# Scores of an attention block: operands of three bf16 parts, two heads per 128 rows, transposed scores as tiles of 64 rows

## The reference, cut to what matters

```python
Q = rope((x @ qw).reshape(b, s, 16, 8)); K = rope((x @ kw).reshape(b, s, 16, 8)); V = (x @ vw).reshape(b, s, 16, 8)
score = einsum('bhqd,bhkd->bhqk', Q, K) / sqrt(8) - 1e10 * (1 - causal)
weights = softmax(score - max(score))
x = layernorm(x + einsum('bhqk,bhkd->bhqd', weights, V).reshape(b, s, 128) @ ow)
gates = top-2 softmax of (x @ router_w + router_b)
x = layernorm(x + sum over experts e of gates[e] * ((silu(x @ w1[e]) * (x @ w3[e])) @ w2[e]))
```

## Time and profile before

| | |
|---|---|
| median of 3 runs | 478.48 us (477.96 to 478.5) |
| profiled execution | 479.53 us, its span 477.8 us |
| mean granted clock of TensorE | 0.955 |
| PE (TensorE matmul) busy | 444.2 us, 93% of the span |
| DVE (VectorE) busy | 318.8 us, 67% |
| ACT (ScalarE) busy | 276.5 us, 58% |
| POOL (GpSimd) busy | 167.2 us, 35% |
| chain that ended last | PE 75%, DVE 8%, ACT 5%, DMA 5%, issue 4% |

### The profile page before, as it was taken

The page is one execution under the profiler, slowest core; times in us unless marked ns, Lnnn a source line. Parts: engine busy times, 40 slices in busy tenths (PEclk is TensorE's granted clock), DMA queues, the critical chain, the costliest instruction groups (busy, mean ns, idle before and its releaser), DMA issues.

```text
span 477.8 us, 7339 instructions
## 1 busy us (share of the span) xinstructions
PE 444.2 (93%) x2340; PEld 278.9 (58%) x2340; DVE 318.8 (67%) x1059; ACT 276.5 (58%) x512; POOL 167.2 (35%) x167
## 2 busy tenths in 40 slices
PE   5877999999999999999999998989999999999991
PEld 2345555555545544545555544448887788788780
DVE  3889957777787787776867873314656756756753
ACT  1212056765766766757757656956566565665560
POOL 4514020240411502404205022026656555665661
PEclk9976579999999999999999999999999999999996
DMA  7977610312112303112122000000000000000000
GB/s 242 279 208 201 164 20 4 106 21 66 45 21 67 62 1 96 30 38 72 20 69 43 1 1 1 2 0 2 0 1 1 23 1 1 23 2 1 22 1 22
DMA packets 41749, 23.64 MB, mean 49 GB/s; under 512 B 31280, under 2 KB 33968, under 8 KB 41712
## 3 DMA queue, kind: packets, MB, share of 16 engines
q1 hardware_dynamic: 41712, 23.18, 17.8%
HBM read 14.26 MB, written 8.65 MB: 48 GB/s over the span
## 4 chain that ended last, share of the span: by engine, by line
PE 75%; DVE 8%; ACT 5%; DMA 5%; issue 4%; SPq 2%; POOL 0%; POOLq 0%; DVEq 0%; ACTq 0%
PE bank L968 16%; PE bank L984 16%; PE bank L1053 15%; PE bank L950 14%; PE bank L1064 7%; DVE maxima L718 3%; ACT num L545 3%; DVE num L777 2%; PE bank L1002 2%; PE bank L907 2%; DMA k_scratch<-rope_lo 2%; DVE num L850 2%; DMA q_scratch<-rope_lo 1%; ACT num L607 1%; SPq L325 1%
## 5 line engine op out<-in xcount | busy, mean ns | idle before, releaser
L545 ACT ACTIVATE num<-bank 128x512 f32<-128x512 f32 (+1 forms) x304 | 159.3, 579 | 98.4 <-PE bank L968 95.8
L950 PE MATMUL bank<-k_op,q_op 128*128 128x512 f32 (+15 forms) x384 | 126.9, 381 | 6.8 <-DMA q_op<-q_scratch 3.5
L968 PE MATMUL bank<-q_op,k_op 128*128 128x512 f32 (+1 forms) x304 | 129.8, 442 | 3.4 <-ACT num L545 2.3
L447 POOL TENSOR_SCALAR_AFFINE_SELECT num<-num 128x512 f32<-128x512 f32 x64 | 40.3, 636 | 214.1 <-ACT num L545 214.1
L718 DVE TENSOR_REDUCE maxima<-bank 128x1 f32<-128x512 f32 x128 | 87.7, 685 | 25.3 <-PE bank L950 24.6
L478 POOL TENSOR_TENSOR q_op<-num,q_op 128x512 fp32r<-128x512 f32 x64 | 82.9, 1299 | 60.4 <-ACT q_op L600 59.2
L950 PEld LDWEIGHTS bank<-k_op,q_op 128*128 128x128 f32 x384 | 76.0, 203 | 40.9 <-DVE maxima L718 23.0
L968 PEld LDWEIGHTS bank<-q_op,k_op 128*128 128x128 f32 x304 | 56.9, 191 | 65.1 <-ACT num L545 36.9
L984 PE MATMUL bank<-num,v_op 128*32 128x512 f32 (+3 forms) x768 | 82.5, 502 | 3.2 <-ACT num L545 2.5
L850 DVE TENSOR_TENSOR num<-bank,num 128x512 f32<-128x512 f32 x64 | 44.2, 691 | 56.9 <-ACT num L607 53.8
L1053 PE MATMUL bank<-q_op,w_hi 128*128 128x512 f32 x256 | 81.5, 400 | 0.4 <-DVE num L850 0.2
(11 more groups left out here) (87 smaller groups left out, 362.2 us busy)
## 6 DMA issues: line engine op xcount, KB each, us to landing
k_op<-k_scratch SPq DMA_DIRECT2D x16, 256.0 KB, 2.8
q_op<-q_scratch SPq DMA_DIRECT2D x64, 52.0 KB
w_raw<-in_w_all SPq DMA_DIRECT2D x6, 512.0 KB, 4.2
q_scratch<-rope_hi SPq DMA_DIRECT2D x8, 256.0 KB, 3.1
k_scratch<-rope_hi SPq DMA_DIRECT2D x8, 256.0 KB, 3.3
xT<-in_x_feat SPq DMA_DIRECT2D x4, 256.0 KB, 5.6
k_scratch<-k_op SPq DMA_DIRECT2D x2, 512.0 KB, 5.9
q_scratch<-rope_lo SPq DMA_DIRECT2D x4, 256.0 KB, 3.5
```

The source lines that it names most:

```text
L545: act.activation(num[:, t % PB, h:h + heads, off:CH], t_bank[k % TB][:, 0:heads * (CH - off)].rearrange("p (h t) -> p h t", h=heads), ACT. ...
L950: pe.matmul(s_bank[k % SB][:, 0:width], q_op[u][:, j, :, :].rearrange("p h q -> p (h q)"), k_op[u][:, lo:lo + width], start=True, stop=Tru ...
L968: pe.matmul(t_bank[k % TB][:, 0:heads * (CH - off)].rearrange("p (h j q) -> p h j q", h=heads, q=QD), k_op[w][:, kt * P:(kt + 1) * P], q_o ...
```

## The change

Q and K are kept in three bf16 parts. A head's operand has six products of parts, 48 rows, and three rows for the maximum; two heads stand on 128 rows (64 rows each), and a group of four heads takes two such pairs.

- The opening: for a chunk ScalarE rounds part 0, VectorE takes the rest in place, ScalarE rounds part 1 of the chunk before (`second_part`), GpSimd takes part 2 of the chunk two before (`third_part`). SP issues six stores of half the size for a chunk instead of three, and waits for part 0, 1 and 2 in turn. `load_k` has two DMAs instead of one. A memset of GpSimd moves behind its second chunk.
- S: 48 units again, 64 queries of two heads each; 17,408 columns in a stage instead of 16,896. Their banks, that of MROWS and that of NORM are now one ring of three (jobs, `JOB`, `ring`).
- T: a unit is 2 or 4 matmuls of 64 rows, the two heads of a pair on rows 0 to 63 and 64 to 127 and in two neighbouring banks; 20 units and 48 matmuls in a stage instead of 38 and 38. Two such double banks instead of three single ones. ScalarE takes one exponential of up to 1024 columns for a unit.
- PV: as before, one tile at a time; the buffers for its input are four instead of three.
- The split of the maxima, now in three parts, moves from VectorE to GpSimd, as five dependent operations; MROWS is a bf16 matmul.
- The plan's constants are set anew for the smaller number of T units.

```diff
-NB = CH // QD
+NPR = 2
+HR = P // NPR
+QB = P // NPR
+NB = CH // QB
 KT = S // P
-QROWS = 3 * DH + 2
-KROWS = 3 * DH
+Q_PART = (0, 0, 1, 1, 2, 0)
+K_PART = (0, 1, 0, 1, 0, 2)
+PARTS = 3
+KROWS = len(Q_PART) * DH
+QROWS = KROWS + PARTS
...
-S_UNITS = [(0, j, 0) for j in range(CH // QD)]
-S_UNITS += [(1, j, half) for j in range(CH // QD, S // QD) for half in range(2)]
+S_UNITS = [(j // NB, pr, j, half) for j in range(S // QB) for pr in range(NPR) for half in range(j // NB + 1)]
...
-    return CH // (CH - t_off(c, kt))
+    return 2 if CH - t_off(c, kt) > CH // 2 else GH
...
-TB = 3
+TB = 2
 HB = 4
-PB = 3
+PB = 4
...
-S_LATE, S_EARLY = 0, 3
-MROWS_AT, NORM_AT, MROWS0_AT, NORM0_AT = 5, 9, 18, 21
-PV_LAG, PV_LAG_LAST = 3, 6
+S_LATE, S_EARLY = 0, 2
+MROWS_AT, NORM_AT, MROWS0_AT, NORM0_AT = 2, 4, 9, 11
+PV_LAG, PV_LAG_LAST = 2, 3
...
+        job_bank = [low[0], low[1], small_bank]
+
+        def ring(s, step):
+
+            return small_bank if s == GROUPS else job_bank[JOB[s, step] % SB]
...
+                for part in range(PARTS):
+                    sp.wait_ge(part_ready[part], n + 1)
+                    for r, of in enumerate(K_PART if is_k else Q_PART):
+                        if of == part:
+                            sp.dma_start(dram[heads, r * DH:(r + 1) * DH, cols], rope_part[part][:, n % 2, :])\
+                                .then_inc(parts_stored[n % 2], 16)
...
+            def third_part(n):
+                pool.wait_ge(part_ready[1], n + 1)
+                if n >= 2:
+                    pool.wait_ge(parts_stored[n % 2], STORES * 16 * (n // 2))
+                pool.tensor_tensor(rope_part[2][:, n % 2, :], roped[:, n % 2, :], rope_part[1][:, n % 2, :],
+                                   ALU.subtract).then_inc(part_ready[2], 1)
 
             for n in range(2 * CHUNKS):
+                if n >= 2:
+                    third_part(n - 2)
                 pool.wait_ge(turned, n + 1)
                 if n >= 2:
-                    pool.wait_ge(lo_ready, n - 1)
+                    pool.wait_ge(part_ready[2], n - 1)
                 pool.tensor_tensor(roped[:, n % 2, :], by_cos[:, n % 2, :], by_sin[:, n % 2, :], ALU.add)\
                     .then_inc(roped_ready, 1)
-            pool.memset(flat[1].bitcast(F32), 0.0).then_inc(ops_filled, 1)
...
+            def split_max(s, c):
+
+                first = 5 * (NC * s + c)
+                top = maxima[:, 0, :, c * NB:(c + 1) * NB]
+
+                def then(ins, k):
+                    ins.then_inc(split_step, 1)
+                    pool.wait_ge(split_step, first + k)
+
+                if c > 0:
+                    pool.wait_ge(max_joined, s + 1)
+                else:
+                    pool.wait_ge(job_read, SB + last_score(s, c) + 1)
+                part = max_part[c]
+                then(pool.tensor_scalar(neg_max[:, :, :], top, -1.0, None, ALU.mult), 1)
+                then(pool.tensor_copy(part[:, :, 0, :], neg_max[:, :, :]), 2)
+                then(pool.tensor_tensor(rest[:, :, :], neg_max[:, :, :], part[:, :, 0, :], ALU.subtract), 3)
+                then(pool.tensor_copy(part[:, :, 1, :], rest[:, :, :]), 4)
+                then(pool.tensor_tensor(part[:, :, 2, :], rest[:, :, :], part[:, :, 1, :], ALU.subtract), 5)
+                pool.sem_inc(max_split, 1)
+
...
+            def second_part(n):
+                act.wait_ge(rest_ready, n + 1)
+                if n >= 2:
+                    act.wait_ge(parts_stored[n % 2], STORES * 16 * (n // 2))
+                act.activation(rope_part[1][:, n % 2, :], roped[:, n % 2, :], ACT.Copy).then_inc(part_ready[1], 1)
 
             for n in range(2 * CHUNKS):
+                if n == 4:
+                    act.wait_ge(ld_small, 16 * 2)
+                    act.activation(ident_b[:, :], ident[:, :], ACT.Copy).then_inc(ident_cast, 1)
                 if n in (PROJ_FIRST - 1, PROJ_FIRST + 1):
                     copy_v((n - PROJ_FIRST + 1) // 2)
                 act.wait_ge(roped_ready, n + 1)
                 if n >= 2:
-                    act.wait_ge(hilo_stored[n % 2], 3 * 16 * (n // 2))
-                act.activation(rope_hi[:, n % 2, :].bitcast(F32R), roped[:, n % 2, :], ACT.Copy)\
-                    .then_inc(hi_ready, 1)
+                    act.wait_ge(parts_stored[n % 2], STORES * 16 * (n // 2))
+                act.activation(rope_part[0][:, n % 2, :], roped[:, n % 2, :], ACT.Copy).then_inc(part_ready[0], 1)
+                if n >= 1:
+                    second_part(n - 1)
...
+            def first_rest(n):
+                dve.wait_ge(part_ready[0], n + 1)
+                dve.tensor_tensor(roped[:, n % 2, :], roped[:, n % 2, :], rope_part[0][:, n % 2, :], ALU.subtract)\
+                    .then_inc(rest_ready, 1)
...
+                        each = heads // 2
+                        act.activation(num[:, t % PB, :, off:CH].rearrange("p (k i) t -> p i k t", i=2)[:, :, h:h + each, :],
+                                       t_bank[k % TB][:, :, 0:each * (CH - off)]
+                                       .rearrange("p i (k t) -> p i k t", k=each),
                                        ACT.Exp, scale=scale).then_inc(t_exped, 1)
...
                     if step[0] == "S":
-                        _, c, j, half = step
-                        k = S_UNITS.index((c, j, half))
+                        _, c, pr, j, half = step
                         once(q_loaded[u][c], turn_u * (16 * GH), ("q", c))
-                        once(k_loaded[u][half], turn_u * 16, ("k", half))
+                        once(k_loaded[u][half], turn_u * (16 * NPR), ("k", half))
                         lo = half * CH
-                        width = min(CH, QD * (j + 1) - lo)
-                        pe.wait_ge(s_reduced, NS * s + k + 1)
-                        pe.matmul(s_bank[k % SB][:, 0:width], q_op[u][:, j, :, :].rearrange("p h q -> p (h q)"),
-                                  k_op[u][:, lo:lo + width], start=True, stop=True).then_inc(s_ready, 1)
+                        width = min(CH, QB * (j + 1) - lo)
+                        pe.wait_ge(job_read, JOB[s, step] + 1)
+                        pe.matmul(ring(s, step)[:, 0:width], q_op[u][:, pr, j, :, :].rearrange("p i q -> p (i q)"),
+                                  k_op[u][:, pr, lo:lo + width], start=True, stop=True).then_inc(job_ready, 1)
...
-                        pe.matmul(t_bank[k % TB][:, 0:heads * (CH - off)].rearrange("p (h j q) -> p h j q", h=heads, q=QD),
-                                  k_op[w][:, kt * P:(kt + 1) * P],
-                                  q_op[w][:, c * NB + off // QD:(c + 1) * NB, h:h + heads, :]
-                                  .rearrange("p j h q -> p h j q"), start=True, stop=True)\
-                            .then_inc(t_ready, 1)
+                        each = heads // 2
+                        width = CH - off
+                        for pr in range(h, h + each):
+                            for i in range(2):
+                                rows = slice(i * HR, (i + 1) * HR)
+                                ins = pe.matmul(t_bank[k % TB][:, i, (pr - h) * width:(pr - h + 1) * width]
+                                                .rearrange("p (j q) -> p j q", q=QB),
+                                                k_op[w][rows, pr, kt * P:(kt + 1) * P],
+                                                q_op[w][rows, pr, c * NB + off // QB:(c + 1) * NB, i, :],
+                                                start=True, stop=True, tile_position=(i * HR, 0))
+                        ins.then_inc(t_ready, 1)
```

286 lines of the change are left out of this document (139 added, 147 removed).

## The result

| | before | after |
|---|---|---|
| median | 478.49 us | 499.03 us (497.89 to 499.7) |
| ratio | | 1.0427, 95% interval 1.0403 to 1.0451 |
| span of the profiled execution | 477.8 us | 496.2 us (execution 497.89) |
| first transposed product | 58.71 us | 85.56 us |
| distance of equal points of a stage | 32.11 us | 31.2 us |

The change makes the kernel 4.3% slower, and the forecast of 497.0 was 2 us off. The parts of it were much further off and made up for each other. Of the 18.4 us between the spans, the opening gave +26.85 (predicted +14.5), the seven stages from the first transposed product to the value product that ends the last of them -7.05 (predicted +5), and the rest -1.4 (predicted -1).

A forecast was written before the change was run, and what follows sets the result against it. The prediction took TensorE, in its written order, as the bound (30.3 of 32.1 us a stage). It summed 478.5 + 14.5 (opening) + 5 (seven stages) - 1 (last stage) = 497 us, own range 488 to 507, overall 464 to 512.

The forecast's parts named there:

- Part one, the serial chain: Opening: part 0 waits for stores of the chunk two before, through GpSimd's part 2; 5.96 us a chunk.
- Part one, SP's loads, "+3.5": Opening: group 0's loads on SP's queue twice hold up the next chunk's stores; 3.5 us added, chunk 7 at 55.2.
- Part one, the end of the opening: VectorE's rest of chunk 7 precedes the last 28 score units (14.3 us); last maximum near 71, some 12.5 later.
- Its other line, by SP's queue: Opening: last store issued near 60, two more K loads in between, so the first transposed product comes 16 us later.
- part 0 every 6 us: Written sign for the opening: ScalarE's part 0 comes every 6 us, with a wait for the store ahead of it.
- Part two, the stages, "+0.7": TensorE, per stage: products -3.5, scores +0.2, weight loads -0.5, 28 more tiling changes +4.5; seven stages +5 us.
- the new order leaves as much time: Each stage: rows of maxima need 2.58 us of SP issue, and the new order leaves as much time for it.
- same stalls as now: Each stage: transposes take a score unit's place in the shared three-bank ring four times; stalls stay at 1.8 us.
- Rival A: Stages: row tiles need no drain, weights load ahead; 28.9 us a stage, 467 us in all; chance 0.27.
- rival B: Stages: products on halves of the rows don't run together; 36 us a stage, 525 us in all; chance 0.10.
- Part two, the split, "0 to 0.5": Each stage: GpSimd's five small operations for the split of the maxima just fit; 0 to 0.5 us a stage.
- Part three, "-1": Last stage: tiling changes +3.7, products -3.5, fewer exponentials about -1; -1 us in sum, experts unchanged.

The follow-up runs named there:

- 52-row run: The changed kernel with Q loads of 52 rows instead of 51, the added row being zeros: 482.98 us, ratio 1.0084.
- full-row run: The changed kernel with transposed products on the full 128 rows, the other head's rows of Q zero, 24 tiling changes a stage: 502.42 us, ratio 1.0487.
- clustered order: The changed kernel with score products moved behind the second transposed unit in five tiles, 42 tiling changes a stage instead of 52: 503.46 us, ratio 1.0511.
- other order of the queues: Kernel with both edits, SP's group loads and five small loads moved later, first product for rows of maxima 15 scores later: 473.38 us, ratio 0.9874.
- both edits: The changed kernel with Q loads of 52 rows and ScalarE's part 1 right behind part 0 of a chunk: 477.79 us, ratio 0.9962.
- last experiment: The kernel with the other order of the queues, and ScalarE also issues the stores of part 0: 473.51 us, ratio 0.988.
- both edits and ScalarE's stores: The kernel with both edits, and ScalarE's own DMA queue issues the stores of part 0: 478.76 us, ratio 0.9978.

## Why the prediction was right, and where it was not

**Direction and time.** Right, and the range held the time. But the sum was right by luck, through errors of +12.35, -12.05 and -0.4 us that cancel.

**Part one, the serial chain.** Its form was right (part 0 waits for the stores of the chunk two before), its period was not: 4.8 to 5.2 us instead of 5.96. Of the terms, the landing was too dear (3.44 was taken for stores of before; here the last store of a chunk lands in 2.4) and GpSimd's part 2 takes 1.15 instead of 1.26. To shorten it by the other order (part 1 behind part 0) was worth some 4 us.

**Part one, SP's loads, "+3.5".** This is the step that failed. The price of a load was carried over from loads of 26 rows to loads of 51; it doubled, and the block at the two loads cost 5.0 and 6.6 us over a plain period of 4.8. With 52 rows it costs 2.1 and 3.5 (part 0 at 30.70, 37.62 and 45.98), so half of it is the row count, and the other half alone is more than the 3.5, for which the prediction gave no working. The forecast of chunk 7's part 0 at 55.2 was nearly met (56.24) by a period that was too long and loads that were too cheap. The 52-row run gives the whole term: 16 us of the result hang on that one row, 12.6 in the opening and some 3 in the stages (7 x 0.45).

**Part one, the end of the opening.** The prediction had VectorE's rest of chunk 7 ahead of the last 28 scores, and took the last maximum for 71; it came at 79.5. It overlooked two waits. VectorE's rest of chunk 7 stands behind a maximum whose score TensorE does behind a projection of V, and starts at 60.24, 3.4 us after part 0 is done. And TensorE's product for the first rows of maxima stands ahead of 27 of these scores in its queue, and waits for a split that GpSimd does behind its part 2 of chunk 7 (4.64 us idle). Its other line, by SP's queue, had the right mechanism and gave +16 instead of +26.85: from the end of the last store's issue to the rows of maxima SP took 15.1 us (64.31 to 79.41) where it had taken 8.0, and this, not the last maximum, set the first transposed product. The written test "if the opening ends before 66 us, part one is wrong" was passed; "part 0 every 6 us" was not.

**Part two, the stages, "+0.7".** Measured: -0.9. Two terms were mis-sized. A change of tiling costs 0.11 us, not 0.16, so 28 changes are 3.1 and not 4.5. And the 0.6 that was left for the second product's weights isn't there: 0.32 for a 512-wide pair is streaming and one change. With -4.1 for the products, +0.2, -0.5 and +3.1 the sum is -1.3. The rest is the late rows of maxima: "the new order leaves as much time" was wrong by 0.45, by the loads of 51 rows in front of them; without them (52 rows) the stage is 30.75, -1.36, near the sum. That this proves every term would be too much said. No run isolates the -0.5 for shorter weight loads. And "same stalls as now" was wrong: with 52 rows TensorE's busy time (by its modelled ends) is 2.83 us less than before (28.67 against 31.50) and its idle time 1.47 more (2.08 against 0.61); 1.7 of the 2.08 are waits for VectorE to free a bank, of which there were none before. Rival A (no drain, 28.9) is out by the full-row run and by the product behind a pair, whose start is 0.11 us later than the streaming of the pair; rival B (36) by the 0.32 us for two 512-wide products and the 0.54 for four. The rule of the Trainium skill, TensorEngine Tiling (Array Packing), section Tiling Modes, that a change of tiling mode drains TensorE, agrees with what these runs show for tiles of 64 rows, 0.11 us a change. The written sign of it is there too: the weights behind a pair are not loaded while it runs. Whether the 0.11 is the draining or the load of 0.10 that nothing hides any longer was not told apart.

**Part two, the split, "0 to 0.5".** Right for what was priced (the move of before's split: 0.0), and blind for what mattered: with the split left on VectorE a stage is 2.4 us longer, 13.7 us in all, by waits on the ring and by the fall of the clock behind them. The ring of three banks has no slack: the clustered order lost through it as well.

**Part three, "-1".** Measured -1.4, again as a sum of two larger numbers. The part that changed lasts from the last product of rows of maxima to the first product of the experts. By stretch for before, for the changed kernel, and for the run with the other order of the queues, which does there the same work:

```profile
288.06:316.82 28.76, 24.76 (x167) 11.30 (x165) 8.12 (x35) 21.70 (x45) 6.10 (x9) 1.00 0.01 1
308.03:335.36 27.33, 23.02 (x176) 8.50 (x176) 8.91 (x35) 19.89 (x28) 6.12 (x9) 0.88 0.01 2
284.36:308.78 24.42, 19.98 (x176) 7.68 (x176) 8.91 (x35) 19.86 (x28) 6.10 (x9) 1.00 0.01 2
```

At full clock the stretch is 4.3 us shorter than before, where the prediction had -1; at a mean clock of 0.88 it is 2.9 us longer than that. At 308 to 310 us TensorE was busy 0.78 of 2 us, waiting for ScalarE's copies (1.19 before 309.73), and the granted clock went to 0.50, the lower level of 1.2 GHz, at 312 to 314; it fell once more, to 0.50 at 325 to 327. The value product of 512 columns at 313.07 took 1.75 us instead of 1.06. The prediction had named such a fall, guessed some 5 us for it and left it out of the sum. The profiles show the fall with 52 rows, with part 1 behind part 0, with both edits and with the last experiment (26.97 to 27.33 us for the stretch), and not with the other order alone or with both edits and ScalarE's stores (24.42 each). So some 2.6 to 2.9 us between two of these kernels can be this fall alone.

**Open.** Why the last stage gains 4.3 us at full clock, rather than 1, was not taken apart. How much of the 5.4 us that the opening is still longer than before lies in its half clock (0.50 from 57 to 64 us) was not tried; VectorE is busy 6.89 of these 7 us.

## What to carry to other kernels

A DMA's price is carried over only with its shape: look at the divisors of its slowest dimension, and pad a prime or an awkward count by a row of zeros. When a part of a chain grows, list for every queue what is written behind the instruction that now waits; here one row count and the places of a few instructions turned a loss of 4.3% into a gain of 1.3%. When a sum of terms meets the time, check the terms one by one all the same.

## What the runs showed of the hardware

- The time for which SP is held by the issue of a load of 512 two-byte columns: 0.45 us at 52 rows, 1.0 at 51, 3.1 at 53; a following load of 128 rows, itself unchanged, takes 0.45, 0.85 and 2.19.
- A change between the full array and 64-row tiles costs 0.10 to 0.11 us in each direction with bf16 weights, whose load takes 0.10 us instead of 0.19 for four bytes.
- Two products on different halves of the rows, into neighbouring banks, run fully together: 0.32 us for two of 512 columns with the change of tiling behind them, 0.54 for four.
- After TensorE had waited 1.28 us for a bank inside a stage (up to 201.56), the granted clock was 0.53 of full speed from 203 to 205 us, and a value product took 1.86 us instead of 0.99.
- Five dependent operations on 128x16 elements cost VectorE 1.0 us (0.17 each, 0.21 apart) and GpSimd 1.4 us; on GpSimd they lay beside other work.
